# dt in the state-space scan of the feed-forward stage: three exact bf16 parts stacked in 96 partitions and spread by one bf16 product, in place of one f32 product

## Chip, cores and metric

The kernel runs on one core of a Trainium2 chip. The time is the device time of one launch in microseconds (us); of the kernel before there are three runs, and one more execution that the hardware profiler recorded. A lower time is better.

## What is computed

The program is a two-layer post-norm decoder on four sequences of 512 positions and 512 features. Each layer has a mixer, a cross step and a feed-forward part, each followed by a layer norm. Two things matter here: the gated feed-forward part of layer 0 and the selective scan in the cross step of layer 1. The scan doesn't depend on layer 0's feed-forward part, so the kernel runs the two in one stage.

```python
def _L0_ffn_ref(x, w_gate, w_up, w_down):
    gate = jnp.einsum('bsd,hd->bsh', x, w_gate)
    up = jnp.einsum('bsd,hd->bsh', x, w_up)
    gated = jax.nn.silu(gate) * up
    return jnp.einsum('bsh,dh->bsd', gated, w_down)

def _L1_xattn_ref(hidden_states, z, ...):
    ...
    dt = jax.nn.softplus(dt + dt_proj_b[None, :, None])
    A = -jnp.exp(A_log)
    ...
    def step(state, inp):
        d, b, c, u = inp
        dA = jnp.exp(d[..., None] * A)
        state = state * dA + (d * u)[..., None] * b[:, None, :]
        y = jnp.einsum('bdn,bn->bd', state, c)
        return (state, y)
    ...
    y = y + D[None, :, None] * x
    y = y * silu(z)
    return jnp.swapaxes(y, 1, 2)
```

In the scan there are 512 channels, 16 states for each, and 512 positions. dt is f32, all other factors of the scan too.

## The kernel before

A batch is a sequence of blocks; between two of them stands a barrier of all engines, and at the end of some groups of blocks their semaphores are cleared. Everything but the scan's own operations and the spreads is computed with products of bf16 halves: `product` (lines 297, 300 and 301) multiplies high by high, high by low and low by high.

The block that the change touches is `hidden_and_scan`. It is built nine times: once at the start for a scan alone, in each batch once as `ffn` (16 hidden tiles, and the scan of layer 1, `which == 1`), once as `moe` (33 hidden tiles, in three of them with the scan of layer 0 for the next batch). In the `ffn` block the 512 channels of the scan are J = 4 column blocks of 128 partitions. A step s takes 32 of these channels: rows 32 (s % 4) and on, of column block s // 4. There are 16 of them (`blocks`), numbered from 0. 32 channels by 4 states fill the 128 partitions, and the other 4 states lie in the free dimension (GRP = 4), so a step's operations are 128 x 2048.

What a step of the scan does, by engine and line:

- TensorE spreads 32 rows over 128 partitions by a product with a 0/1 pattern (`headmean`, which holds 1/16; the 16 is taken back in scale factors): `spread_dt` (L876) for dt and `spread_dtx` (L889) for dt times x. Both are f32 products with 32 rows of contraction. L876 writes `dt_bank`, L889 writes `dtx_bank`.
- ScalarE (`decays`, L997) makes four exponentials of 511 columns from `dt_bank` into one of two `da` buffers, with the state's rate as scale.
- VectorE (`inputs`, L1054) multiplies the spread dtx by the B rows, and `scan` (L1064) runs the recurrence over 128 x 2048.
- GpSimd (L1154) multiplies the scanned states by the C rows. Each fourth step TensorE sums over the states (`reduce_quad`, L898) and VectorE takes the sum (`finish_y`, L1069).

Beside it a step does one hidden tile: TensorE's `gate` and `up` (12 bf16 products each), ScalarE's tanh (`gate_curve`, L1022), and on VectorE the gate (L1074), times up (L1082) and the low half (`low_part`, L283). From step 4 on TensorE adds a `down_piece` of 12 products, and VectorE takes it out of its bank (`take_down`, L1102 and L1105). All but the last four pieces use the one bank 7, so a piece waits until the one before is taken.

The order on TensorE is written out by hand:

```python
for step in range(steps):
    if 2 <= step + 1 < blocks:
        spread_dtx(step + 1)
    if step + 2 < blocks and not carried:
        spread_dt(step + 2)
    ...
    if step + 1 < tiles:
        gate(step + 1)
        up(step + 1)
```

then `reduce_quad` and the down piece. The dt spread of step s waits for the exponentials of s - 1 (`decay`), since there is one bank for it; the dtx spread waits for the inputs of s - 1 (`inp`). ScalarE's exponentials for step s wait until scan s - 2 is over. VectorE's order in a step is scan, inputs of the next step, the down piece, `finish_y`, gate, times up, low half. Ahead of the loop VectorE splits x into halves (L283, four operations) and makes the inputs of step 0. SP does one thing here: it loads weight slots into a ring of three (L168), each as soon as a slot is free.

Of the kernel before, what the change touches and what calls it, by code (L numbers as in the profile page):

```python
# [285 lines left out]
def halves(region):  # L286

    return region.bitcast(BF16)
# [21 lines left out]
def stream_block(k, sp, slots_end, last=NSLOTS):  # L310
    k.w.load_until(sp, slots_end, RING - 1, last)
# [474 lines left out]
def hidden_and_scan(nc, k, tag, tiles, slot, which, gated, last, splitter=None, early=()):  # L786
# [14 lines left out]
    with ExitStack() as ctx:  # L801
# [41 lines left out]
        def quartet(s):  # L843
            return states(s).rearrange("p (n t) -> p n t", n=GRP)

        carried = gated and blocks > 0
        made = 1 if carried else 0

# [13 lines left out]

        @blk.sync
        def _(sp):
            stream_block(k, sp, slot + (hidden_slots(tiles) if tiles else 0), last)
            if splitter:
                splitter.move(sp)

        @blk.tensor
        def _(pe):  # L870
            def spread_dt(s):

                if s >= 1:
                    pe.wait_ge(decay, s)
                at = slice(32 * (s % 4), 32 * (s % 4) + 32)
                pe.matmul(dt_bank, k.headmean[at, :], dt[at, s // 4, :], start=True, stop=True).then_inc(dt_mm, 1)  # L876

# [107 lines left out]
        def _(act):  # L985
# [29 lines left out]
            def gate_curve(jt):  # L1015
# [5 lines left out]
                else:  # L1021
                    act.activation(t2[jt % 2], gate_bank(jt), ACT.Tanh, scale=0.5).then_inc(th, 1)  # L1022

            if blocks and not made:
                decays(0)
            if tiles:
                gate_curve(0)
            for step in range(steps):
# [19 lines left out]
        def _(dve):  # L1048
# [60 lines left out]
            if tiles and not gated:  # L1109
                for c in range(KM):  # L1110
                    low(dve, xlo[:, c, :], k.xr[:, c, :]).then_inc(xsplit, 1)
            if blocks:
                inputs(0)
            for step in range(steps):
                if step < blocks:
                    scan(step)
                    for n in split_now(step, 1):
                        if not splitter.by_pe(n):
                            splitter.low_part(dve, n)
                if step + 1 < blocks:  # L1120
                    inputs(step + 1)
                if LAG <= step < pieces + LAG:
                    take_down(step - LAG)
                if step % 4 == 1 and 5 <= step <= blocks + 1:
                    finish_y(step // 4 - 1)
                if step < tiles and not gated:
                    silu_gate(step)
                if step < tiles:
                    times_up(step)
                if gated and step < tiles:  # L1130
                    times_weight(step)
                if step < tiles:
                    low_part(step)
                if carried and step == 1:
                    half = slice(J // 2, J)
                    dve.tensor_tensor(dt[:, half, :], dt[:, half, :], dtx[:, half, :], ALU.add).then_inc(late_sum, 1)
                if which == 0 and step % 4 == 2 and step + 2 < blocks:
                    inputs_of(step // 4 + 1)
# [973 lines left out]
def set_constants(nc, k, params_src, squares_src, loads):  # L2112

    with ExitStack() as ctx:
# [25 lines left out]
        def _(dve):  # L2140
# [2 lines left out]
                dve.tensor_copy(k.key_rows_b[:, q, :], k.key_rows[q])  # L2143
            dve.tensor_scalar(k.minus, k.ident, -1.0, None, ALU.mult)
            dve.tensor_scalar(k.stack, k.headmean[:, 0:32], 16.0, None, ALU.mult)
            dve.tensor_copy(k.identb, k.ident).then_inc(neg, 1)
            dve.wait_ge(rate, 1)
            dve.tensor_scalar(k.a0, k.a0, -16.0, None, ALU.mult)
# [31 lines left out]
def decoder(nc, xT, guwT, ctxT, wstream, params, squares, out):  # L2180

    with ExitStack() as ctx:
# [63 lines left out]
        k.ident, k.meanmat, k.headmean = [k.squares[:, i, :] for i in range(3)]  # L2246
        k.key_sum, k.key_rows = [[k.squares[:, 3 + 2 * i + q, :] for q in range(2)] for i in range(2)]
        k.identb = sb("identb", [P, P], BF16)
        k.stack = sb("stack", [P, 32], BF16)
        k.minus = halves(k.held[:, 0, 0:P // 2])  # L2250
        def param(name):
# [228 lines left out]
```

## Time and profile before

| | before |
|---|---|
| median of three runs | 3989.97 us (3979.78 to 3990.33) |
| the profiled execution's own time | 3982.17 us |
| its span, first to last instruction | 3980.4 us |
| mean granted TensorE clock | 0.939 of full speed |
| busy share: TensorE, VectorE, ScalarE, GpSimd | 88%, 80%, 40%, 35% |
| matmuls recorded | 15,442 |

The profile gives for each instruction its start and duration, and in brackets the idle time of its engine before it with what ended that. Matmuls overlap (the next starts before the last ends), so for TensorE the distance from start to start is what one costs, and the end of its records is modelled. An f32 product appears as two records. The engines' queues run in the order of the program; a wait holds up what stands behind it on that engine.

### The profile page before, as it was taken

To read this page: it belongs to the slowest core of one execution; us is meant where nothing else is said; L and a number is where in the kernel's file an instruction comes from. 1 tells how busy PE (TensorE), PEld (TensorE's weight loads), DVE (VectorE), ACT (ScalarE), POOL (GpSimd) and SP (SyncE) were. 2 spreads that over 40 slices of the span, in tenths; PEclk is the share of its full clock that TensorE was granted. 3 is DMA by queue.
4 is the path that set the end of the run, shared out by engine and by line. 5 is a ranking of instruction groups with operands and counts; after the bars stand their busy time and mean duration, and the time that the engine had idled before them with its cause. 6 is when DMAs were issued, how large, how long until landed. Compare 5 with 4: busy or idle time off the path is not lost. (4 is left out here: it accounts for less than half of the span.)

```text
span 3980.4 us, 41707 instructions
## 1 busy us (share of the span) xinstructions
PE 3521.7 (88%) x15442; PEld 1475.8 (37%) x15442; DVE 3172.7 (80%) x2733; ACT 1609.0 (40%) x2189; POOL 1378.0 (35%) x493
## 2 busy tenths in 40 slices
PE   5777779989999979989999979989999988967999
PEld 1222243334333443334333443334433443324444
DVE  5999469887999869887999869887999869895333
ACT  5666343214655353214655353214655343213001
POOL 3454304362344304372344304372344304361000
PEclk9788899999899999989899999989899999978999
DMA  6678402121233302122233302122233302110222
GB/s 228 241 286 302 159 12 72 60 78 65 88 105 97 131 27 72 59 72 72 85 102 102 130 27 72 57 74 72 79 104 105 131 27 72 57 40 16 103 96 72
DMA packets 105431, 382.95 MB, mean 96 GB/s; under 512 B 14224, under 2 KB 27920, under 8 KB 102800
## 3 DMA queue, kind: packets, MB, share of 16 engines
q1 hardware_dynamic: 83632, 342.57, 24.6%
q10 hardware_dynamic: 21600, 37.73, 3.4%
q8 instruction: 125, 2.05, 0.2%
q14 instruction: 74, 0.61, 0.1%
HBM read 290.80 MB, written 64.32 MB: 89 GB/s over the span
## 5 line engine op out<-in xcount | busy, mean ns | idle before, releaser
L300 PE MATMUL ps<-r,ring 128*128 128x512 bf16 (+1 forms) x2040 | 781.4, 384 | 0.0
L297 PE MATMUL ps<-xr,ring 128*128 128x512 bf16 x1568 | 613.8, 391 | 1.4 <-PEq L2278 1.4
L301 PE MATMUL ps<-xr,ring 128*128 128x512 bf16 x1568 | 611.1, 390 | 0.0
L297 PE MATMUL ps<-r,ring 128*128 128x512 bf16 (+3 forms) x1384 | 545.4, 395 | 49.4 <-DVE xc L1102 17.8
L301 PE MATMUL ps<-r,ring 128*128 128x512 bf16 (+3 forms) x1384 | 544.8, 395 | 0.0
L1154 POOL TENSOR_TENSOR hh<-hh,bc 128x2048 f32<-128x2048 f32 x72 | 334.7, 4649 | 518.3 <-DVE hh L1064 518.3
L1154 POOL TENSOR_TENSOR bc<-bc 128x2048 f32<-128x2048 f32 x64 | 304.3, 4754 | 344.6 <-DVE bc L1064 344.6
L1154 POOL TENSOR_TENSOR r<-r,bc 128x2048 f32<-128x2048 f32 x56 | 260.9, 4658 | 297.7 <-DVE r L1064 297.7
L1064 DVE TENSOR_TENSOR_SCAN hh<-da,hh 128x2048 f32<-128x2048 f32 x72 | 325.7, 4523 | 1.3
L1105 DVE TENSOR_TENSOR xc<-xc,ps 128x512 f32<-128x512 f32 x176 | 119.5, 679 | 226.1 <-PE ps L301 225.8
L1064 DVE TENSOR_TENSOR_SCAN bc<-da,bc 128x2048 f32<-128x2048 f32 x64 | 296.0, 4625 | 0.5
L300 PEld LDWEIGHTS ps<-r,ring 128*128 128x128 bf16 (+1 forms) x2040 | 196.9, 97 | 246.2 <-issue 13.2
L1064 DVE TENSOR_TENSOR_SCAN r<-da,r 128x2048 f32<-128x2048 f32 x56 | 261.0, 4660 | 0.6
L997 ACT ACTIVATE da<-da,params_sb 128x511 f32<-128x511 f32 x372 | 248.0, 714 | 31.0 <-DMA da<-r 23.9
L297 PEld LDWEIGHTS ps<-xr,ring 128*128 128x128 bf16 x1568 | 151.8, 97 | 271.6 <-issue 106.5
L997 ACT ACTIVATE da<-ps,params_sb 128x511 f32<-128x511 f32 x384 | 231.8, 692 | 23.4 <-DVE r L1064 10.1
L297 PEld LDWEIGHTS ps<-r,ring 128*128 128x128 bf16 (+3 forms) x1384 | 134.0, 97 | 284.8 <-issue 136.1
L301 PEld LDWEIGHTS ps<-xr,ring 128*128 128x128 bf16 x1568 | 151.4, 97 | 208.0 <-issue 6.4
L307 PE MATMUL ps<-identb 128*128 128x512 bf16 x748 | 183.0, 401 | 30.9 <-ACT r L1427 22.1
L997 ACT ACT_TABLE_LOAD x98 | 125.7, 1283 | 198.7 <-issue 178.0
L301 PEld LDWEIGHTS ps<-r,ring 128*128 128x128 bf16 (+3 forms) x1384 | 134.4, 97 | 186.2 <-issue 11.7
L889 PE MATMUL ps<-ctxTs,squares_sb 32*128 32x512 f32 x256 | 153.8, 682 | 52.5 <-DVE ctxTs L1058 21.8
(267 smaller groups left out, 6559.4 us busy)
## 6 DMA issues: line engine op xcount, KB each, us to landing
ring<-wsplit SPq DMA_DIRECT2D x216, 768.0 KB, 4.2
r<-wstream SPq DMA_DIRECT2D x54, 768.0 KB, 7.0
ring<-wsplit SPq DMA_DIRECT2D x76, 512.0 KB, 3.9
wsplit<-ring SPq DMA_DIRECT2D x38, 768.0 KB, 4.3
da<-r ACTq DMA_DIRECT2D x360, 63.9 KB, 2.1
wsplit<-r SPq DMA_DIRECT2D x14, 768.0 KB, 5.5
r<-wstream SPq DMA_DIRECT2D x19, 512.0 KB, 6.4
r<-xT SPq DMA_DIRECT2D x7, 1024.0 KB, 6.4
```

The costliest lines, as they stand in the source:

```text
L297: mm = pe.matmul(out, w_hi, x_hi, start=start, stop=False)
L300: pe.matmul(out, w_hi, x_lo, start=False, stop=False)
L301: return pe.matmul(out, w_lo, x_hi, start=False, stop=stop)
L307: pe.matmul(k.ps[:, bank, :], k.identb, k.identb[:, None, :].broadcast_to([P, 4, P]), start=True, stop=True)
L889: pe.matmul(dtx_bank, k.headmean[at, :], source, start=True, stop=True).then_inc(dtx_mm, 1)
L997: return act.activation(k.da[s % 2][:, n, 1:T], source, ACT.Exp, scale=rate[:, GRP * s + n:GRP * s + n + 1])
L1064: dve.tensor_tensor_scan(states(s), k.da[s % 2][:, :, :].rearrange("p n t -> p (n t)"), states(s), 0.0, ALU.mult, ALU.add).then_inc(scanne ...
L1105: dve.tensor_tensor(k.xc[:, m, :], k.xc[:, m, :], down_bank(p), ALU.add).then_inc(taken, 1)
L1154: pool.tensor_tensor(quartet(s), quartet(s), k.out_rows, ALU.mult).then_inc(read, 1)
```

## The change

In the `ffn` block alone (`stacked`), dt of the column blocks 1 to 3 (steps 4 to 15) is split into three bf16 parts whose sum is the f32 value. ScalarE copies it to bf16, VectorE subtracts that in place from dt, ScalarE copies the rest to bf16, VectorE subtracts again, and the last rest is the third part. SP then issues twelve transfers within SBUF that lay the three parts of each group of 32 rows under each other in 96 partitions (`dt_stack`). From step 4 on `spread_dt` is one bf16 product over these 96 rows with a bf16 copy of the pattern. The first four steps keep their f32 product. SP's stream of weights is cut in two around the transfers. `dt_parts` and `dt_stack` lie in a region that is free in this block.

```diff
@@ hidden_and_scan
+        stacked = which == 1
+        dt_parts, stack_in = sem("dt_parts"), sem("stack_in")
         carried = gated and blocks > 0
...
         @blk.sync
         def _(sp):
+            if stacked:
+                stream_block(k, sp, slot + 1, last)
+                sp.wait_ge(dt_parts, 4)
+                for i in range(3):
+                    for c in range(4):
+                        sp.dma_start(k.dt_stack[32 * i:32 * i + 32, :, c, :], k.dt_parts[32 * c:32 * c + 32, i, :, :]).then_inc(stack_in, 16)
             stream_block(k, sp, slot + (hidden_slots(tiles) if tiles else 0), last)
...
             def spread_dt(s):
                 if s >= 1:
                     pe.wait_ge(decay, s)
+                if stacked and s >= 4:
+                    if s == 4:
+                        pe.wait_ge(stack_in, 12 * 16)
+                    pe.matmul(dt_bank, k.headmean_b[0:96, :], k.dt_stack[:, s // 4 - 1, s % 4, :], start=True, stop=True).then_inc(dt_mm, 1)
+                    return
                 at = slice(32 * (s % 4), 32 * (s % 4) + 32)
                 pe.matmul(dt_bank, k.headmean[at, :], dt[at, s // 4, :], start=True, stop=True).then_inc(dt_mm, 1)
...
+            if stacked:
+                act.activation(k.dt_parts[:, 0, :, :], dt[:, 1:J, :], ACT.Copy).then_inc(dt_parts, 1)
             if blocks and not made:
                 decays(0)
+            if stacked:
+                act.wait_ge(dt_parts, 2)
+                act.activation(k.dt_parts[:, 1, :, :], dt[:, 1:J, :], ACT.Copy).then_inc(dt_parts, 1)
             if tiles:
                 gate_curve(0)
...
+            if stacked:
+                dve.wait_ge(dt_parts, 1)
+                dve.tensor_tensor(dt[:, 1:J, :], dt[:, 1:J, :], k.dt_parts[:, 0, :, :], ALU.subtract).then_inc(dt_parts, 1)
             if blocks:
                 inputs(0)
+            if stacked:
+                dve.wait_ge(dt_parts, 3)
+                dve.tensor_tensor(k.dt_parts[:, 2, :, :], dt[:, 1:J, :], k.dt_parts[:, 1, :, :], ALU.subtract).then_inc(dt_parts, 1)
             for step in range(steps):
@@ set_constants, decoder
+            dve.tensor_copy(k.headmean_b, k.headmean)
...
+        k.headmean_b = sb("headmean_b", [P, P], BF16)
+        k.dt_parts = halves(r0[:, 1536:3840]).rearrange("p (i j t) -> p i j t", i=3, t=T)
+        k.dt_stack = halves(r0[0:96, 8192:11264]).rearrange("p (j c t) -> p j c t", c=4, t=T)
```

How it moves the queues. In the rows below L numbers of the changed program are its own: L902 is the old L889, L886 the new product, L1072 and L1082 are the old L1054 and L1064, L1010 is the old L997.

ScalarE, start of the `ffn` block (`da` are the decays, `row` and `r0` behind L1022/L1035 the tanh), before:

```order
L984 UNCONDITIONAL_BRANCH
L997 ACT_TABLE_LOAD
L997 ACTIVATE da0<-ps,params_sb 128x511 x4
L1022 ACTIVATE row<-ps 128x512
L997 ACTIVATE da1<-ps,params_sb 128x511 x4
```

and in the change:

```order
L997 UNCONDITIONAL_BRANCH
L1038 ACTIVATE r0<-r1 128x1536
L1010 ACT_TABLE_LOAD
L1010 ACTIVATE da0<-ps,params_sb 128x511 x4
L1043 ACTIVATE r0<-r1 128x1536
L1035 ACTIVATE row<-ps 128x512
L1010 ACTIVATE da1<-ps,params_sb 128x511 x4
```

The first copy stands ahead of the table load, the second between the first four exponentials and the first tanh.

VectorE at the same place (`hh0` is the first states buffer; the scan stands as SCALAR_TENSOR_TENSOR), before:

```order
L1047 UNCONDITIONAL_BRANCH
L283 TENSOR_TENSOR r0<-xr 128x512 x4
L1054 TENSOR_TENSOR hh0<-ps,bc 128x2048
L1064 SCALAR_TENSOR_TENSOR hh0<-da0,hh0 128x2048
L1054 TENSOR_TENSOR hh1<-ps,bc 128x2048
```

and in the change:

```order
L1065 UNCONDITIONAL_BRANCH
L283 TENSOR_TENSOR r0<-xr 128x512 x4
L1132 TENSOR_TENSOR r1<-r1,r0 128x1536
L1072 TENSOR_TENSOR hh0<-ps,bc 128x2048
L1137 TENSOR_TENSOR r0<-r1,r0 128x1536
L1082 SCALAR_TENSOR_TENSOR hh0<-da0,hh0 128x2048
L1072 TENSOR_TENSOR hh1<-ps,bc 128x2048
```

One subtraction stands ahead of the inputs of step 0 and one between them and the first scan.

TensorE at the top of step 2 of the first `ffn` block, before:

```order
L301 MATMUL ps<-xr,ring 128x512
L889 MATMUL ps<-r,squares_sb 128x512
L876 MATMUL ps<-r,squares_sb 128x512
L297 MATMUL ps<-xr,ring 128x512
L300 MATMUL ps<-r,ring 128x512
```

and in the change:

```order
L301 MATMUL ps<-xr,ring 128x512
L902 MATMUL ps<-r,squares_sb 128x512
L886 MATMUL ps<-r,headmean_b 128x512
L297 MATMUL ps<-xr,ring 128x512
L300 MATMUL ps<-r,ring 128x512
```

The new product stands where the f32 one stood, behind the dtx spread and ahead of the gate tile; so it is in each of the steps 2 to 13.

## Rows read from the trace of the kernel before

**Rows 1.** Timeline, VectorE, start of the second ffn block; columns: start, duration, engine, line, shapes

```profile
1497.09 2.50 DVE L283 TENSOR_TENSOR r<-xr 128x512 bf16<-128x512 f32 x4 [2.28 <-PEq L2278]
1500.87 2.29 DVE L1054 TENSOR_TENSOR hh<-ps,bc 128x2048 f32<-128x2048 f32 x1 [1.29 <-PE ps L889]
1503.27 4.42 DVE L1064 TENSOR_TENSOR_SCAN hh<-da,hh 128x2048 f32<-128x2048 f32 x1
```

**Rows 2.** Timeline, ScalarE, the same place

```profile
1497.05 1.28 ACT L997 ACT_TABLE_LOAD   x1 [4.26 <-PEq L2278]
1499.17 2.42 ACT L997 ACTIVATE da<-ps,params_sb 128x511 f32<-128x511 f32 x4 [0.83 <-PE ps L876]
```

**Rows 3.** Timeline, VectorE, steps 1 and 2: inputs, and the two low halves

```profile
1518.11 2.29 DVE L1054 TENSOR_TENSOR bc<-ps,bc 128x2048 f32<-128x2048 f32 x1 [0.86 <-PE ps L889]
...
1521.75 0.69 DVE L283 TENSOR_TENSOR held_first<-r 128x512 bf16<-128x512 f32 x1
...
1530.31 1.67 DVE L283 TENSOR_TENSOR held_first<-r 128x512 bf16<-128x512 f32 x1
```

**Rows 4.** Timeline, GpSimd, steps 1 and 2

```profile
1517.32 4.57 POOL L1154 TENSOR_TENSOR hh<-hh,bc 128x2048 f32<-128x2048 f32 x1 [4.96 <-DVE hh L1064]
1526.86 4.58 POOL L1154 TENSOR_TENSOR bc<-bc 128x2048 f32<-128x2048 f32 x1 [4.97 <-DVE bc L1064]
```

**Rows 5.** Timeline, TensorE, its waits for VectorE in steps 4, 6 and 7

```profile
1538.56 0.69 PE L889 MATMUL ps<-r,squares_sb 32*128 32x512 f32 x1 [0.87 <-DVE r L1054]
...
1568.14 0.39 PE L297 MATMUL ps<-r,ring 128*128 128x512 bf16 x1 [0.49 <-DVE xc L1102]
...
1577.70 0.39 PE L297 MATMUL ps<-r,ring 128*128 128x512 bf16 x1 [0.23 <-DVE xc L1102]
```

**Rows 6.** Timeline, VectorE, its waits in steps 9 and 13

```profile
1594.44 2.29 DVE L1054 TENSOR_TENSOR r<-ps,bc 128x2048 f32<-128x2048 f32 x1 [0.56 <-PE ps L889]
...
1634.76 2.29 DVE L1054 TENSOR_TENSOR bc<-ps,bc 128x2048 f32<-128x2048 f32 x1 [1.70 <-PE ps L889]
```

**Rows 7.** Timeline, TensorE, a stand in the mixing block and that of step 15

```profile
948.87 0.39 PE L297 MATMUL ps<-r,ring 128*128 128x512 bf16 x1 [2.08 <-POOL held_first L283]
...
1654.94 0.39 PE L297 MATMUL ps<-r,ring 128*128 128x512 bf16 x1 [2.96 <-DVE xc L1105]
```

**Rows 8.** Timeline, TensorE, both spreads in step 6 and the next product

```profile
1561.08 0.69 PE L889 MATMUL ps<-r,squares_sb 32*128 32x512 f32 x1
1561.09 0.69 PE L876 MATMUL ps<-r,squares_sb 32*128 32x512 f32 x1
...
1562.14 0.40 PE L297 MATMUL ps<-xr,ring 128*128 128x512 bf16 x1
```

**Rows 9.** Timeline, TensorE, mixture stage: dtx alone, a 96-row bf16 product, the next

```profile
1984.43 1.12 PE L889 MATMUL ps<-ctxTs,squares_sb 32*128 32x512 f32 x2
1985.49 0.39 PE L943 MATMUL ps<-r,stack 96*128 96x512 bf16 x1
1985.72 0.39 PE L297 MATMUL ps<-xr,ring 128*128 128x512 bf16 x1
```

**Rows 10.** One line's instructions, durations in ns min/median/max: copies and subtractions up to 1,536 columns

```profile
L260 ACT ACTIVATE ring<-r x52: 622/1475/1527, 12.7 to 420.9; 128x1536 bf16<-128x1536 f32 x38, 128x1024 bf16<-128x1024 f32 x11, 128x1152 bf16<-128x1152 f32 x1, 128x512 bf16<-128x512 f32 x1
...
L265 DVE TENSOR_TENSOR r<-r x5: 1192/1726/1727, 129.3 to 376.7; 128x1536 bf16<-128x1536 f32 x4, 128x1024 bf16<-128x1024 f32 x1
```

**Rows 11.** Timeline, TensorE, both spreads in step 2

```profile
1523.84 0.69 PE L889 MATMUL ps<-r,squares_sb 32*128 32x512 f32 x1
1524.24 0.69 PE L876 MATMUL ps<-r,squares_sb 32*128 32x512 f32 x1
```

**Rows 12.** Stretches: length, busy PE, PEld, DVE, ACT, POOL, granted clock, DMA share, GB/s

```profile
1655.70:1658.90 3.20, 3.20 (x9) 1.03 (x8) 3.17 (x2) 0.00 (x0) 3.13 (x1) 0.50 0.58 177
...
949.10:952.40 3.30, 3.30 (x9) 1.12 (x8) 3.30 (x4) 0.00 (x0) 2.67 (x3) 0.50 0.58 194
```

**Rows 13.** Timeline, SP, eight transfers of 32 rows within SBUF

```profile
1907.46 5.03 SPq L1843 DMA_DIRECT2D da<-r  x8
```

## Prediction

> **What bounds the kernel now.** I read the page's busy shares first, then the timelines of single engines in the second batch's feed-forward stage (1497 to 1674 us), then the granted clock by stretches. The shares have TensorE and VectorE both high, and in this stage both are nearly full, so they don't say on which of the two a microsecond counts. The timelines do. The program has four batches with one such stage each, and what is worked out for one is taken four times.
>
> At the start VectorE splits x until 1499.59, idles 1.29 us for the dtx spread, makes the inputs at 1500.87 and starts its first scan at 1503.27 [rows 1]. ScalarE's four exponentials are done by 1501.59 [rows 2].
>
> In steps 0 to 4 VectorE and GpSimd set the pace. In step 1 VectorE waits 0.86 us for TensorE's spread, in step 2 it doesn't, yet the remainder (line 283) ends 5.12 us after the start of GpSimd's product in both: 1522.44 against 1517.32, 1531.98 against 1526.86 [rows 3, 4]. GpSimd starts when the scan ends and its 4.57 us close the step; without a wait the remainder only stands longer (1.67 us instead of 0.69). The Trainium skill says so of this pair (SBUF — State Buffer, section "SBUF: two separate sides"): the port pair that they share is an exclusive lock, held for a whole instruction. The trace agrees. So a later first scan is not won back from that 0.86 us.
>
> TensorE is early by then: in step 4 it waits 0.87 us for VectorE's inputs, until 1538.56. In steps 6 and 7 it waits for the down bank, 0.49 and 0.23 us by the brackets, which is 0.66 and 0.41 against the regular 0.22 us between bf16 starts; the last such wait ends at 1577.70 [rows 5]. From there TensorE runs without a gap and VectorE waits for its dtx spread, 0.56 us in step 9 and 1.70 us in step 13 [rows 6]. Then VectorE leads: TensorE stands 2.96 us, until 1654.94, for VectorE to take the piece before [rows 7], and runs the last pieces. The stage's end is thus a chain: VectorE's first scan; VectorE's pace to 1577.70; TensorE's pace to step 13; VectorE's pace to 1654.94; TensorE's rest.
>
> **The spread that is replaced costs nothing.** In a steady step dtx (L889) and dt (L876) start at 1561.08 and 1561.09, and the next bf16 product at 1562.14: 1.06 us for both [rows 8]. In the mixture stage, where only dtx is spread, it takes 1.06 us too: 1984.43 to 1985.49 [rows 9]. The two read different groups of 32 rows and run side by side. The bf16 product over 96 rows that comes in has its like right there: L943, 96 rows, behind a lone dtx, 0.23 us to the next start at 1985.72 [rows 9]. So dtx plus bf16 dt is 1.29 where dtx plus f32 dt was 1.06: **TensorE loses 0.23 us in a steady step**. Bounds: 0 (it runs beside dtx after all) and 0.5 (half of the pair's 1.06).
>
> Which of the twelve count? Those of steps 2 and 3 come before TensorE's wait of step 4. That of step 13 comes before its 2.96 us stand. Those of steps 4 to 7 are counted below. Those of steps 8 to 12 lie on TensorE's stretch of the chain: 5 x 0.23 = 1.15 us.
>
> **The split at the start.** ScalarE now copies 1,536 columns ahead of its table load; this copy takes 1.48 us in the weight split [rows 10]. 1497.05 + 1.48 + 1.28 + 2.42 = 1502.23 [rows 2], second copy to 1503.71. VectorE gets one subtraction of 1,536 columns before the inputs and one after, 1.73 us each at that length [rows 10]: 1499.59 + 1.73 + 2.29 = 1503.61, a wait to 1503.71, + 1.73 = 1505.44, where the scan starts instead of at 1503.27. **2.15 us per stage**; by VectorE's sum alone, 3.46 added less 1.29 idle filled, 2.17. Bounds: 1.7 (queued instructions overlap) and 2.8 (three handovers at 0.2 more). TensorE needs none of it before step 2, and from step 4 on waits for VectorE's inputs, so the whole 2.15 goes through.
>
> **The wait that grows.** TensorE's steps 1 to 3 do not move, so its wait in step 4 becomes 0.87 + 2.15 = 3.0 us, and 0.3 more since the 0.40 us by which dt now starts late in steps 2 and 3 [rows 11] no longer lengthens the pair. After the 2.96 us stand at the end the granted clock reads 0.50, the lower of the two levels (1.2 GHz), from 1655.7 to 1658.9; after a 2.08 us idle at 948.87 it is 0.50 from 949.1 to 952.4 [rows 7, 12]. So I expect this level after step 4 as well, for the same 3.3 us. At half clock 3.3 us do the work of 1.65: TensorE is 1.65 late. The bf16 dt adds 0.23 in each of steps 4 to 7, 0.92, less 0.3 in step 4, where dt starts late on its wait as in step 2. Against this stand the losses of steps 5 to 7, 0.22 (too small to be listed), 0.66 and 0.41: 1.65 + 0.92 - 0.3 - 1.29 = 1.0 us late at the start of TensorE's stretch. Bounds: 0 (clock stays up; the 0.6 left is covered) and 2.0. VectorE's two waits grow by it: 0.56 to 1.7 in step 9, and together by 2.1 at step 13.
>
> **The transfers.** SP waits for the fourth count (1505.4), then issues 12 transfers. Eight of its 32-row transfers take 5.03 us to issue [rows 13]: 12 x 0.63 = 7.6, to 1513.0. I give 2 to 4 us for landing; TensorE wants them at 1524.24 [rows 11]. Slack of 7 us or more: nothing. Behind the waiting SP stands the next weight load; its slot comes free only in step 0 of TensorE and its tile is used two steps later, so a microsecond there costs nothing.
>
> Elsewhere a 128x128 copy among the constants and one more semaphore clear at some group ends: 0.4 us in all, a guess, bounds 0 and 1.
>
> **Sum.** Per stage 2.15 + 1.15 + 1.0 = 4.3; 4 x 4.3 + 0.4 = 17.6. The profiled execution took 3982.17 us and would take 3999.8. It is 7.8 below the median of the three runs, 3989.97, which spread over 10.5 us. On the median: **4007.6 us**, +0.44%. A measurement tells about 0.3%, 12 us, from no change.
>
> **Rivals.**
> - *The clock stays up in step 4.* Then 4 x 3.3 + 0.4 = 13.6, 4003.6. For it: a wait of 0.87 there leaves no trace. Against: rows 7 and 12. Chance 0.15.
> - *One price only.* If the 0.23 is hidden beside dtx and the clock stays: 4 x 2.15 + 0.4 = 9.0, 3999.0. If the later scan is swallowed by VectorE's waits of 0.86, 0.56 and 1.70: 5.0, 3995.0. Against: the equal 5.12 us of rows 3 and 4, and that the later two waits are for TensorE, which itself follows VectorE in step 4. Chance 0.14.
> - *The other side: the f32 spread was not free.* If the pair's costs add up in the steps that count, a dt product falls from 1.06 to 0.23, 0.83 less: 4.15 per stage over five steps, 10 over all twelve. Less 2.15: -2.0 or -7.8 per stage, 3982.0 or 3958.8. It decides once dt beyond dtx costs over 0.23 + 2.15 / 5 = 0.66 us. For it: in step 2 dt starts 0.40 us behind dtx [rows 11]; nothing waits for that. Against: rows 8 and 9. The Trainium skill (FP8 and Floating Point Precision, section "TensorE Precision Notes") has true FP32 at 4 passes through the array. By that rule, as an estimate, three passes of 0.22 are saved, 0.67 x 5 less 2.15, the stage gains 1.2 and the time is 3985; it counts passes, not what runs beside them. Chance 0.05.
> - *The stack comes late.* Its runs of 1 KB go to few rows while weights are in flight. Beyond 7 us of delay each further microsecond is paid in each stage, once step 4's wait of 3 us is used up: 13 us late is 4 x 3 = 12 more, 4020. Chance 0.08.
>
> **Chances.** The forecast has the rest, 0.58, all but 0.06 of it beyond 12 us. First rival 0.10 slower, 0.05 same. Second 0.14 same. Third 0.04 faster, 0.01 same. Fourth 0.08 slower. Sums: slower 0.70, same 0.26, faster 0.04. The range reaches down to one price and an execution as low as the profiled one (3993) and up by the bounds of the start (2.8) and of the clock (2.0) to 4017.
>
> **What would show it.** Right: first scan of each stage 2.1 us later against the stage's start; L902/L886 1.29 us to the next product; step 1 without its wait, step 13's at 3.8 us; a granted clock of 0.50 in step 4 behind an idle of 3 us. Wrong: L886 starting with L902; a stage no longer than now; TensorE idle in step 2.

## The result, and the profile after

The change is slower. Its median over five runs is 4012.14 us (4005.19 to 4017.06) against 3989.01 us of five runs of the kernel before (3979.78 to 3990.33): a ratio of 1.0062, 95% interval 1.0044 to 1.0080. 4007.6 was forecast, with a range from 3993 to 4017.

| | after |
|---|---|
| the profiled execution's own time, its span | 4012.14 us, 4010.4 us |
| mean granted TensorE clock | 0.933 |
| busy share: TensorE, VectorE, ScalarE, GpSimd | 89%, 80%, 40%, 34% |
| matmuls recorded | 15,394 |

The timeline of VectorE at the start of the second `ffn` block, which answers [rows 1]:

```profile
1509.72 2.50 DVE L283 TENSOR_TENSOR r<-xr 128x512 bf16<-128x512 f32 x4 [2.28 <-PEq L2306]
1512.13 1.75 DVE L1132 TENSOR_TENSOR r<-r 128x1536 f32<-128x1536 f32 x1
1513.80 2.28 DVE L1072 TENSOR_TENSOR hh<-ps,bc 128x2048 f32<-128x2048 f32 x1
1516.32 1.76 DVE L1137 TENSOR_TENSOR r<-r 128x1536 bf16<-128x1536 f32 x1 [0.23 <-ACT r L1043]
1517.99 4.42 DVE L1082 TENSOR_TENSOR_SCAN hh<-da,hh 128x2048 f32<-128x2048 f32 x1
```

The first scan stands 8.27 us behind the start of the block, where it stood at 6.18: 2.09 later, in all four stages.

The same place on ScalarE (answers [rows 2]):

```profile
1509.70 1.48 ACT L1038 ACTIVATE r<-r 128x1536 bf16<-128x1536 f32 x1 [4.28 <-PEq L2306]
1511.20 1.28 ACT L1010 ACT_TABLE_LOAD   x1
1512.49 2.42 ACT L1010 ACTIVATE da<-ps,params_sb 128x511 f32<-128x511 f32 x4
1514.79 1.50 ACT L1043 ACTIVATE r<-r 128x1536 bf16<-128x1536 f32 x1
```

The copies take 1.48 and 1.50 us, near the 1.475 of [rows 10]; the second ends after VectorE's inputs and makes it wait 0.23 us. SP's queue issues the transfers right after (answers [rows 13]):

```profile
1518.11 8.36 SPq L872 DMA_DIRECT2D r<-r  x12
```

TensorE: the first new product, in step 2, and a wait in step 3, both of the second `ffn` block; then step 4 of the first and of the second block (answers [rows 5] and [rows 8]):

```profile
1537.54 0.39 PE L886 MATMUL ps<-r,headmean_b 96*128 96x512 bf16 x1
...
1543.73 1.12 PE L902 MATMUL ps<-r,squares_sb 32*128 32x512 f32 x2 [0.47 <-DVE bc L1072]
...
649.35 1.12 PE L902 MATMUL ps<-r,squares_sb 32*128 32x512 f32 x2 [2.73 <-DVE r L1072]
650.40 0.39 PE L886 MATMUL ps<-r,headmean_b 96*128 96x512 bf16 x1
650.63 0.39 PE L297 MATMUL ps<-xr,ring 128*128 128x512 bf16 x1
...
1553.25 1.12 PE L902 MATMUL ps<-r,squares_sb 32*128 32x512 f32 x2 [2.74 <-DVE r L1072]
```

The pair takes 1.05 + 0.23 = 1.28 us to the next product, where it took 1.06. The first new product starts at 1537.54 behind its dtx spread, with no wait in brackets; the last of the transfers was issued by 1526.47, and each landed 2.1 to 2.9 us after it was issued: the stack is not late. The stand of step 4 grew from 0.87 to 2.74 in the second block, and step 3, which had no wait there, now waits 0.47. Behind the stand of step 4 the granted clock falls in the first, third and fourth block, not in the second. Stretches just behind the two stands (columns as in [rows 12]):

```profile
650.00:653.40 3.40, 3.40 (x11) 1.14 (x10) 3.37 (x3) 0.00 (x0) 1.73 (x1) 0.67 0.38 99
...
1553.90:1557.30 3.40, 3.40 (x16) 1.36 (x15) 3.37 (x3) 0.00 (x0) 1.74 (x1) 1.00 0.40 90
```

VectorE's waits in steps 9 and 13 of the first block (0.57 and 1.70 there before, as in the second block in [rows 6]):

```profile
706.36 2.29 DVE L1072 TENSOR_TENSOR r<-ps,bc 128x2048 f32<-128x2048 f32 x1 [1.71 <-PE ps L902]
...
747.52 2.29 DVE L1072 TENSOR_TENSOR bc<-ps,bc 128x2048 f32<-128x2048 f32 x1 [2.56 <-PE ps L902]
```

I cut both programs at the starts of their blocks, the first VectorE instruction behind each barrier. The four stages, in us:

| | start to first scan | first to last scan | from there to the end | stage |
|---|---|---|---|---|
| before, each of four | 6.18 | 146.54 to 146.57 | 24.98 | 177.70 to 177.73 |
| after, batch 1 | 8.27 | 148.48 | 24.74 | 181.49 |
| batch 2 | 8.27 | 147.59 | 24.93 | 180.79 |
| batch 3 | 8.27 | 148.50 | 24.79 | 181.56 |
| batch 4 | 8.27 | 148.47 | 24.55 | 181.29 |

The stages hold 14.3 us of the change (725.1 against 710.9); 17.2 was forecast. The spans differ by 30.0. The rest, 15.7, lies outside these stages, where the change adds only a 128x128 copy among the constants and a semaphore clear at some group ends. The experiments are about both parts.

### The profile page after: what moved, and what is told of

Same layout as the page of the kernel before. It is cut to its first block and busy times, and to the rows that moved or that the text cites. A ratio compares the mean times of both kernels' runs of the same rounds, so it can differ in the third digit from the quotient of the medians.

```text
span 4010.4 us, 41698 instructions
## 1 busy us (share of the span) xinstructions
PE 3556.4 (89%) x15394; PEld 1487.1 (37%) x15394; DVE 3200.1 (80%) x2742; ACT 1620.4 (40%) x2197; POOL 1344.6 (34%) x493
## 5 line engine op out<-in xcount | busy, mean ns | idle before, releaser
L1082 DVE TENSOR_TENSOR_SCAN hh<-da,hh 128x2048 f32<-128x2048 f32 x72 | 325.6, 4522 | 0.8
L1082 DVE TENSOR_TENSOR_SCAN bc<-da,bc 128x2048 f32<-128x2048 f32 x64 | 296.1, 4627 | 0.5
L1082 DVE TENSOR_TENSOR_SCAN r<-da,r 128x2048 f32<-128x2048 f32 x56 | 260.8, 4657 | 0.6
L1010 ACT ACTIVATE da<-da,params_sb 128x511 f32<-128x511 f32 x372 | 248.0, 714 | 25.5 <-DMA da<-r 18.6
L1010 ACT ACTIVATE da<-ps,params_sb 128x511 f32<-128x511 f32 x384 | 231.8, 691 | 26.9 <-DVE bc L1082 14.5
L301 PEld LDWEIGHTS ps<-r,ring 128*128 128x128 bf16 (+3 forms) x1384 | 134.9, 98 | 187.7 <-issue 14.3
L902 PE MATMUL ps<-ctxTs,squares_sb 32*128 32x512 f32 x256 | 153.2, 680 | 54.1 <-DVE ctxTs L1076 25.5
```

The source lines that it names most:

```text
L301: return pe.matmul(out, w_lo, x_hi, start=False, stop=stop)
L902: pe.matmul(dtx_bank, k.headmean[at, :], source, start=True, stop=True).then_inc(dtx_mm, 1)
L1010: return act.activation(k.da[s % 2][:, n, 1:T], source, ACT.Exp, scale=rate[:, GRP * s + n:GRP * s + n + 1])
L1082: dve.tensor_tensor_scan(states(s), k.da[s % 2][:, :, :].rearrange("p n t -> p (n t)"), states(s), 0.0, ALU.mult, ALU.add).then_inc(scanne ...
```

## The experiments

"Stages" is the sum of the four stages in the run's own profile, less the 710.9 us of before; it comes from one execution of each kernel. The ratio is against executions of the kernel before on the same chip, whose medians were 3989.18 (e1 to e4), 3989.54 (e5 to e8) and 3987.49 us (e9 to e12).

| run | median, us | ratio, 95% interval | stages, us |
|---|---|---|---|
| e1 split only | 3996.28 | 1.0018, 1.0010 to 1.0027 | +8.8 |
| e2 product only | 3990.88 | 1.0004, 0.9996 to 1.0012 | +8.3 |
| e3 transfers only | 3997.65 | 1.0024, 1.0014 to 1.0033 | +0.2 |
| e4 the change again | 4011.22 | 1.0062, 1.0047 to 1.0078 | +15.8 |
| e5 no dt product | 3984.82 | 0.9990, 0.9981 to 0.9998 | 0.0 |
| e6 both on one group of rows | 4015.53 | 1.0062, 1.0047 to 1.0076 | +23.9 |
| e7 change, stand filled | 3999.77 | 1.0026, 1.0017 to 1.0035 | +12.6 |
| e8 pair early | 3981.87 | 0.9984, 0.9974 to 0.9994 | -3.0 |
| e9 change, no transfers | 4019.15 | 1.0068, 1.0047 to 1.0088 | +14.5 |
| e10 cut only | 3995.26 | 1.0018, 1.0009 to 1.0028 | 0.0 |
| e11 before again | 3988.65 | 1.0002, 0.9993 to 1.0010 | +0.2 |
| e12 pair early, stand filled | 3981.89 | 0.9985, 0.9977 to 0.9994 | -3.5 |

### The parts of the change: e1 to e4

**e1**, the change without transfers and bf16 product; every spread is f32 and reads what the subtraction left.

```diff
-            if stacked:
-                stream_block(k, sp, slot + 1, last)
-                sp.wait_ge(dt_parts, 4)
...
-                if stacked and s >= 4:
...
-                    return
```

> The changed kernel with the two copies and two subtractions left in, but without the transfers, and with the f32 spread of dt back in steps 4 to 15 (it reads what the subtraction left, so the decays are of a rest and not of dt). Theory: first scan of each stage 2.1 us later, TensorE idle 2.7 us in step 4, granted clock 0.50 behind it in most stages (0.9 us more by step 13), scans 0 to 15 together 146.6 or 147.4 us; against before 4 x 2.1 to 4 x 3.0, +8 to +12 us, 0.2 to 0.3%. Rival (the split is swallowed by VectorE's waits): scan 15 no later against the stage's start, +0. Rival (there is a cost outside the stages): blocks between the stages longer than in the kernel before by 10 us in sum.

The first scans stand at 8.27 us as in the change. The scans take 146.90, 146.56, 146.89 and 146.91 us: the fall of the clock behind step 4 is there in three stages, and costs 0.35 where the bf16 product doesn't add to it. The down-bank waits of steps 6 and 7 take up the rest of it.

**e2**, the kernel before with a bf16 product of 96 rows (high halves of dt, so other values are spread) from the product for step 4 on.

```diff
+                if which == 1 and s >= 4:
+                    pe.matmul(dt_bank, k.headmean_b[0:96, :], high(dt[0:96, s // 4, :]), start=True, stop=True).then_inc(dt_mm, 1)
+                    return
```

> The kernel before with one edit: from step 4 on the spread of dt is a bf16 product over 96 rows, of the high halves of whatever lies there (so the decays are wrong ones); no split, no transfers. Theory (the f32 spread was free beside dtx): dtx and dt together 1.29 us instead of 1.06; VectorE's wait in step 13 at 2.7 us instead of 1.7; 1.05 us per stage, +4.2 us, 0.1%. Rival (the f32 spread was paid): stage shorter by 3 us or more, -12 us. Rival (the bf16 product runs beside dtx): no change.

The scans take 148.57 to 148.62 us in three stages, 2.0 more (150.27 in the first), where 1.05 was forecast. VectorE's waits in steps 9 and 13 of the second block are 1.65 and 2.60. The forecast had left out the clock: it falls behind step 4's stand here too, and in all four stages, though the stand is only 1.22 to 1.32 us in three of them (1.84 in the first). The second block:

```profile
1547.10 1.12 PE L892 MATMUL ps<-r,squares_sb 32*128 32x512 f32 x2 [1.24 <-DVE r L1057]
...
1547.90:1551.30 3.40, 3.40 (x9) 1.16 (x9) 3.37 (x3) 0.00 (x0) 1.58 (x1) 0.53 0.33 99
```

So 2.0 is the 1.05 us that the product takes with the clock up (second stage of the change) and about 1.0 for the clock. In the first stage the clock stays low for 6.6 us in place of some 3.3, which gives the 1.7 more. Each of e1 and e2 has a fall of the clock of its own behind step 4, and the change has only one; so their stage costs, 8.8 and 8.3, don't add up to those of the change. The whole run shows nothing of the 8.3: by the medians it is 1.7 us slower than before, with an interval that ends at 1.0012 (4.8 us). Why the rest of this kernel is cheaper in most executions is not known.

**e3**, the kernel before with twelve transfers of the same size behind the first inputs, and TensorE waiting for them at the product for step 4.

```diff
+            if stacked:
+                stream_block(k, sp, slot + 1, last)
+                sp.wait_ge(inp, 1)
+                for i in range(3):
+                    for c in range(4):
+                        sp.dma_start(k.dt_stack[32 * i:32 * i + 32, :, c, :], dt[32 * c:32 * c + 32, 1:4, 128 * i:128 * i + T // 2]).then_inc(stack_in, 16)
...
+                if stacked and s == 4:
+                    pe.wait_ge(stack_in, 12 * 16)
```

> The kernel before with twelve transfers within SBUF of the same shape and size as in the change, at the same time in the stage, and TensorE's wait for them at the dt spread of step 4; nothing reads what they write. Theory: hidden, all scans at the same distances as before, +0 (within 3 us). Rival (transfers or the SP queue cost time, by late weights or inside VectorE's work): +2 us or more per stage, 8 us in all, with TensorE or VectorE waiting in step 2 or 3.

From the first scan on no scan moves by 0.1 us, as expected (the first scan itself stands 0.35 us later in one stage and 0.35 earlier in another), yet the run is 8.5 us slower by the medians, with an interval that excludes nothing happening. At +0 to 3 us this forecast failed, and e9 to e11 follow it up.

**e4**, the changed kernel once more, unchanged.

> The changed kernel once more, unchanged. The stages differ by 14.3 us between the two profiled executions and what lies between the stages by 15.7, in work that the change doesn't touch. Theory (the granted clock ahead of the stages falls differently from execution to execution): the stages again 180.8 to 181.6 us each, but the rest anywhere within 3269 to 3285 us. Rival (the change makes the rest longer): the rest again 3283 to 3287.

The ratio repeats. Its stages took 182.59, 180.84, 181.55 and 181.68 us: the clock stayed up in the second again, and stayed low for longer in the first. The rest took 3276.5 us, against 3285.2 in the change's own profile: the theory, that the rest differs from execution to execution, holds, and its rival (3283 to 3287) falls. This execution, 4004.95 us, is the lowest of its six.

### Was the f32 product free? e5 and e6

**e5**, the kernel before without the dt product from step 4 on.

```diff
+                if which == 1 and s >= 4:
+                    return
...
-                act.wait_ge(dt_mm, s + 1)
+                act.wait_ge(dt_mm, min(s + 1, 4) if which == 1 else s + 1)
```

> The kernel before, with no dt spread at all from the product for step 4 on (ScalarE's exponentials of these steps read the values that the bank still holds, so the output is not the reference's). Theory: dtx and the f32 dt product run side by side, so the f32 dt product costs nothing beyond dtx: a lone dtx to the next product is 1.06 us as before, the stage keeps its 177.7 us within 0.3 us and the time is that of before, +0 to -2 us. Rival (the f32 product is not free): each of the 10 products of steps 4 to 13 gives back up to 0.83 us, those of steps 8 to 12 on TensorE's stretch 4 us per stage, time -8 to -16 us.

**e6**, the kernel before with the dt product on the same 32 rows as the dtx product ahead of it.

```diff
+                if which == 1 and s >= 4:
+                    at = slice(32 * ((s - 1) % 4), 32 * ((s - 1) % 4) + 32)
```

> The kernel before, with the f32 dt product from the one for step 4 on reading the same group of 32 rows as the dtx product ahead of it (so dt of other channels is spread and the output is not the reference's). Theory: the overlap of the pair comes from its two different groups of rows; on one group they run one behind the other, the pair takes about 2.1 us instead of 1.06, and the stage grows by about as much as for five to ten products: the scans, 146.5 us from the first to the last before, take 5 to 9 us more per stage, time +20 to +36 us. Rival (the overlap has another reason, or dt has another price than the chain says): pair stays at 1.06 us and the time is that of before.

TensorE in step 6, e5 first:

```profile
1561.06 1.12 PE L891 MATMUL ps<-r,squares_sb 32*128 32x512 f32 x2
1562.11 0.40 PE L297 MATMUL ps<-xr,ring 128*128 128x512 bf16 x1
```

and e6:

```profile
1566.08 1.12 PE L891 MATMUL ps<-r,squares_sb 32*128 32x512 f32 x2
1567.04 1.02 PE L878 MATMUL ps<-r,squares_sb 32*128 32x512 f32 x2
1567.99 0.40 PE L297 MATMUL ps<-xr,ring 128*128 128x512 bf16 x1
```

dtx alone takes 1.05 us, the pair on two groups of rows 1.06 [rows 8], the pair on one group 1.91. With no dt product at all, every stage keeps its 177.72 or 177.73 us. But that equal length is in part luck. Without the product TensorE is at step 4 earlier, stands 1.66 us there in place of 0.87, and the clock falls behind it in all four stages. The second block of e5:

```profile
1538.40:1541.80 3.40, 3.40 (x9) 1.16 (x9) 3.37 (x3) 0.00 (x0) 1.41 (x1) 0.52 0.49 134
```

TensorE is then 1.3 us behind the kernel before at its next dtx spread, and catches up by step 8, since it has no wait in steps 6 and 7 any more. What shows the price is TensorE's own stretch behind that: from the dtx spread of step 8 to that of step 14 it takes 62.31 us before (1580.45 to 1642.76) and 62.27 in e5 (1579.38 to 1641.65), with six f32 dt products between them or none. Together with e6 this settles it for the steps that count: the product that the change replaces cost nothing, and because it ran on other rows than dtx. e6's 0.85 us a step is 6.1 us a stage. By its median e5 is 4.7 us faster than before, where 0 to 2 was expected; its stages give none of it.

### The clock behind step 4: e7

**e7**, the change with 12 products on bank 7 that only keep TensorE busy, in step 4 ahead of its dtx spread.

```diff
+                if stacked and step == 4:
+                    keep_busy(k, pe, 7, 12)
```

> The changed kernel with 12 small products that only keep TensorE busy, in step 4 ahead of its dtx spread, where TensorE stands 2.73 us for VectorE's inputs. Theory: the stand is what brings the granted clock down behind it in three of the four stages (scans 148.5 us against 147.6 in the stage where it stayed up); without the stand the clock stays at 1.00 there, the scans take 147.6 us in all four stages and the time falls by 3 x 0.9 = 2.7 us, 0 to -6 us measured. Rival (the clock falls there by itself, or its fall is covered by later waits): scans stay at 148.5, time as that of the change, +22 us against before.

The first block of e7, TensorE's timeline in step 4:

```profile
641.20 2.75 PE L307 MATMUL ps<-identb 128*128 128x512 bf16 x12
644.11 1.12 PE L902 MATMUL ps<-r,squares_sb 32*128 32x512 f32 x2 [0.15 <-DVE r L1074]
```

and the stretch behind it, where the change had 0.67:

```profile
645.00:648.40 3.40, 3.40 (x16) 1.46 (x16) 3.37 (x3) 0.15 (x1) 1.49 (x1) 1.00 0.45 125
```

All four stages take 180.87 to 180.89 us, the scans 147.61 to 147.63. So the fall costs 0.9 us a stage where it happens in the change. The split and the product are 2.09 + 1.07 by themselves. But the median fell by 11.4 us against e4, where 0 to 6 was expected, and the stages hold 3.2 of it. The other 8 lie outside again.

### Outside the stages: e9, e10, e11

**e9**, the change with its bf16 product reading the first part where ScalarE wrote it, and no transfers.

```diff
-                        pe.wait_ge(stack_in, 12 * 16)
-                    pe.matmul(dt_bank, k.headmean_b[0:96, :], k.dt_stack[:, s // 4 - 1, s % 4, :], start=True, stop=True).then_inc(dt_mm, 1)
+                        pe.wait_ge(dt_parts, 4)
+                    pe.matmul(dt_bank, k.headmean_b[0:96, :], k.dt_parts[0:96, 0, s // 4 - 1, :], start=True, stop=True).then_inc(dt_mm, 1)
```

> The change without its twelve transfers: the bf16 product of 96 rows reads the first part where ScalarE put it (so dt of wrong rows is spread and the output is not the reference's). In the stages nothing should differ from the change: first scan at 8.27 us, scans 147.6 us where the clock stays up and 148.5 us where it falls behind step 4's stand, together 14 to 16 us more than before. Theory A (the transfers of the change cost nothing on their own, what lies outside the stages comes from the granted clock of each execution): time within 4 us of the change's, +18 to +22 us against before. Theory B (the transfers cost 8 us, as the run with transfers alone says): 8 us less than the change, +13 to +15 us.

**e10**, e3 without its transfers and without TensorE's wait: SP's cut and its wait are left, and the constant.

```diff
+            if stacked:
+                stream_block(k, sp, slot + 1, last)
+                sp.wait_ge(inp, 1)
```

> The kernel before with SP's stream of weights cut in two and SP waiting for the first inputs in between, as in the run with transfers alone, but with no transfer and no wait on TensorE. If the 8.5 us of that run come from the cut, the wait or the added constant, they are here too (+8 us); if they come from the transfers, this kernel has the time of before (+0 us, within 4).

**e11**, the kernel before, unchanged.

> The kernel before, unchanged, for a second profile and for what the comparison makes of no change. Theory (blocks outside the feed-forward stages differ from execution to execution by steps of 1.8 and 3.2 us, with the granted clock): the four stages take 177.7 us each again, some other blocks differ from the first profile by such steps, and the ratio is 1.000 with an interval of about 0.001 to either side. Rival (an execution of one program repeats its blocks, so differences outside the stages belong to the kernel that shows them): all blocks within 0.3 us of the first profile.

Theory B falls: without its transfers the change is no faster. Theory A doesn't hold in its numbers either: e9 should have been 18 to 22 us slower than before, and is 31.7 by the medians, 7 above the change. Its six executions spread over 22 us (4002.73 to 4024.70), and its stages hold 14.5. And the 8 us of e3 are in e10, which moves no transfer. Where do they go? In e11 the stages are those of the first profile within 0.15 us, most blocks within 0.1, but the three before the first `ffn` block are 2.53, 1.33 and 3.31 us longer. Four others differ by 0.8 to 2.3 us, up and down, and nearly cancel. The theory behind e11 holds in this: the blocks move in steps, and with the granted clock; the steps are 1.3, 2.5 and 3.3 us there. The second of the three as a stretch (start:end, length, then as in [rows 12]), in the first profile of before:

```profile
556.20:574.00 17.80, 9.77 (x62) 5.57 (x63) 12.65 (x32) 8.94 (x17) 0.02 (x1) 1.00 0.00 0
```

and in e11:

```profile
557.90:577.00 19.10, 11.79 (x61) 6.97 (x63) 12.65 (x32) 8.92 (x17) 0.02 (x1) 0.82 0.00 0
```

e11's own time, 3989.28, is near before's median, and the change's profiled execution is its median. So these two are the pair to compare: spans 22.9 apart, the medians 23.1. Stages 14.1; the mixture blocks 3.5 (2.1, 0.7, 1.4 and -0.8); the two blocks before the last `ffn` block 5.4. That last place in e11 and in the change:

```profile
3256.40:3274.20 17.80, 9.72 (x62) 5.56 (x64) 12.65 (x33) 8.93 (x17) 0.03 (x1) 1.00 0.01 1
3274.20:3299.80 25.60, 14.29 (x61) 8.36 (x61) 17.59 (x25) 16.20 (x24) 0.36 (x1) 0.83 0.00 0
```

```profile
3270.90:3290.50 19.60, 13.42 (x62) 7.19 (x62) 12.91 (x32) 8.95 (x17) 0.00 (x0) 0.74 0.00 1
3290.50:3319.80 29.30, 17.58 (x61) 10.74 (x61) 17.77 (x25) 16.20 (x24) 0.40 (x1) 0.72 0.00 0
```

In e10 and e3 it is the last mixture block that is longer, by 3.1 us. So it is in e4 (138.8 us against 135.7 in e11), though not in the change's own profile (135.0), which is the same program. Six-us stretches in it, e11 and e10:

```profile
3514.00:3520.00 6.00, 6.00 (x24) 2.23 (x23) 6.00 (x8) 1.18 (x2) 6.00 (x4) 0.82 0.30 117
3520.00:3526.00 6.00, 6.00 (x28) 2.43 (x27) 5.28 (x7) 0.60 (x2) 4.78 (x5) 1.00 0.36 131
3526.00:3532.00 6.00, 5.83 (x27) 2.25 (x27) 6.00 (x8) 3.49 (x7) 3.57 (x3) 1.00 0.16 31
```

```profile
3515.00:3521.00 6.00, 6.00 (x24) 2.26 (x23) 6.00 (x8) 1.20 (x2) 6.00 (x4) 0.85 0.30 115
3521.00:3527.00 6.00, 6.00 (x21) 2.35 (x19) 4.86 (x6) 0.00 (x0) 4.78 (x5) 0.72 0.39 131
3527.00:3533.00 6.00, 5.66 (x21) 1.94 (x21) 4.98 (x7) 1.74 (x3) 2.37 (x3) 0.78 0.00 0
```

Up to the first of the three both are alike; then e11's clock is back at 1.00 and e10's stays low for some 18 us more. So, in these pairs of profiles, what a kernel pays outside the stages is how long the granted clock stays low at such places. Part of that is chance, since it differs between executions of one program. Part seems to belong to the kernel, since e10's interval, 1.0009 to 1.0028 over 12 runs, leaves 1 out. What in e10 sets it (the cut, SP's wait or the constant) wasn't taken apart and stays open.

### A faster version: e8 and e12

**e8**, the kernel before with the pair of spreads of steps 9 and 13 issued ahead of the sum over states in steps 8 and 12.

```diff
+                early_pair = which == 1 and step in (9, 13)
-                if 2 <= step + 1 < blocks:
+                if 2 <= step + 1 < blocks and not early_pair:
                     spread_dtx(step + 1)
-                if step + 2 < blocks and not carried:
+                if step + 2 < blocks and not carried and not early_pair:
                     spread_dt(step + 2)
...
+                if which == 1 and step in (8, 12):
+                    spread_dtx(step + 2)
+                    spread_dt(step + 3)
                 if step % 4 == 0 and 4 <= step <= blocks:
                     reduce_quad(step // 4 - 1)
```

> The kernel before, with the dtx and dt spreads of steps 9 and 13 issued one piece earlier on TensorE, ahead of the sum over states and the down piece of steps 8 and 12. Theory: VectorE's waits of 0.56 us in step 9 and 1.70 us in step 13 are waits for these spreads, on the chain; without them VectorE is ahead and the stage ends up to 2.26 us earlier, time -4 to -9 us. Rival (TensorE's total work sets step 13 to 15 anyway, so what VectorE saves it waits for the down bank or for gate and up): the waits move, the stage keeps 177.7 us, time +0.

e8 is faster than both kernels, 0.9984 of before. The stages give 3.0 us of it. The waits of [rows 6] left step 9 and shrank to 0.39 us in step 13, and most of them came back in steps 10 and 14, as the rival had it. VectorE's timeline in the second block:

```profile
1609.95 2.29 DVE L1058 TENSOR_TENSOR r<-ps,bc 128x2048 f32<-128x2048 f32 x1 [0.22 <-PE ps L889]
...
1650.55 2.29 DVE L1058 TENSOR_TENSOR bc<-ps,bc 128x2048 f32<-128x2048 f32 x1 [1.33 <-PE ps L889]
```

Of 2.26 us 0.43 is won. TensorE's stand of step 15 is 1.92 us in all four stages, where it was 2.96. Behind it the clock stays up in three of them, which gives another 0.43 each; in the first it falls all the same:

```profile
763.90:767.10 3.20, 3.20 (x9) 1.14 (x8) 3.13 (x3) 0.00 (x0) 3.20 (x1) 0.51 0.45 151
```

**e12**, e8 with that stand filled.

```diff
+                if which == 1 and step == 15:
+                    pe.wait_ge(decay, 16)
+                    keep_busy(k, pe, 0, 12)
```

> The kernel before with the pair of spreads early in steps 8 and 12, and with 12 products that only keep TensorE busy in step 15, in the 2.96 us in which it stands for VectorE's take of the down bank. Theory: the granted clock stays at 1.00 behind that stand instead of 0.50 for 3.3 us, each stage ends up to 1.6 us earlier on top of the 0.4 to 0.9 us that the early pair brings: stages about 175.3 us, time -12 to -16 us against before. Rival (VectorE, not TensorE, ends the stage, or the clock falls later instead): stages 176.9 us, time as with the early pair alone, -4 to -8 us.

The clock stays up in all four stages, and each takes 176.81 to 176.85 us, no less than e8's best (176.82). The rival was right in effect, though with another engine: TensorE in step 15 of e8,

```profile
1660.54 0.39 PE L297 MATMUL ps<-r,ring 128*128 128x512 bf16 x1 [1.92 <-DVE xc L1109]
1664.50 0.62 PE L898 MATMUL ps<-hh,squares_sb 128*32 128x512 f32 x2 [1.13 <-POOL bc L1158]
```

With the clock up TensorE is through its piece early and waits 1.13 us for GpSimd's last product. The low clock was hidden behind GpSimd but for 0.43 us.

## Why the prediction was right, and where not

The direction, the three terms of the stage and their places came out. The total, 4012.14, lies in the range, but 8.8 us of it come from a place that the forecast had at 0.4. The range left room for them only because it was wide for other reasons (the start and the clock of step 4), and that is luck. By the bounds that the prediction names, the range would be 3991.2 to 4014.2 and not 3993 to 4017; the result lies in both. Step by step:

- *The split at the start*, 2.15 forecast: 2.09 in each stage of the change, e1 and e7. The second copy made VectorE wait 0.23 us, where 0.10 was forecast. Nothing later won the 2.09 back.
- *The spread that is replaced costs nothing*: e5 and e6 show it, and why. 1.29 against 1.06 was forecast for the pair, 1.28 measured. In steps 2 to 4, where it starts late, the f32 product did hold TensorE up, but ahead of waits that took it in. The product's term was 1.15; it is 1.05 in the second block of the change, 1.07 in e7. The rival that has the f32 product not free is out. The Trainium skill (FP8 and Floating Point Precision, section "TensorE Precision Notes") counts 4 passes for true FP32. One alone takes 1.05 us here and a bf16 product 0.23, 4.6 times less, which is near that count. But the count says nothing of a neighbour on other rows, and the 3985 us by it had the wrong sign.
- *The wait that grows*: 3.0 and 0.3 more was forecast for step 4, with steps 1 to 3 of TensorE unmoved. It is 2.74 there in the second block and 0.47 in step 3, 3.2 together: the sum was right, its place not wholly. VectorE's wait in step 1 is gone, as forecast.
- *The clock*: 1.0 in each stage was forecast; it was 0.9 in three of four stages, and none in the second. The same stand of 2.7 us precedes all four, so its length doesn't decide alone. The other runs say so too: in step 4 the clock fell behind 1.22 us (third block of e2) and not behind 1.34 (first block of e3). The forecast took the fall from what followed stands of 2.08 and 2.96 us; what decides it stays open. VectorE's two waits grew by 2.0 us where the clock fell; 2.1 was forecast in the sum. In the list of what would show it I had put step 13 alone at 3.8 us; it reads 2.56. That line contradicted the sum, which had it right.
- *The transfers*: hidden. 8.36 us of issue for 7.6, 2.1 to 2.9 us of landing for 2 to 4, no wait on TensorE, and e9 is no faster without them.
- *The end of the stage*, which the forecast left as it was: from the last scan to the end the four stages are 0.9 us shorter together (24.98 before, 24.55 to 24.93 now). That is why they hold 14.3 us and not 4 x (2.09 + 1.05) + 3 x 0.9 = 15.3.
- *Elsewhere 0.4 us, a guess, bounds 0 and 1*: this is the step that was mis-sized. Between two executions whose times are near the medians, e11's and the change's, 8.8 us are lost outside the stages, in stretches of low granted clock. Of one pair alone this says little: e4's execution loses nothing there against e11's (3276.5 us both), and is 7 us below the change's median. But over all executions the medians lie 23 us apart and the stages hold 14 to 16, so 7 to 9 is the usual loss. I also took the profiled execution as a fair base and only scaled to the median, though it lay 7.8 us under it. e11 lies 7.1 us above it, and the three blocks before the first stage, with their lower clock, make up 7.2.

So 17.2 + 0.4 was forecast, and 14.1 + 8.8 happened. The stage was 3.1 us too dear and the rest 8.4 too cheap; by the medians that is 0.44% forecast and 0.58% measured (the ratio above says 0.62%).

What stays open: why the change pays more outside than e7, which only adds twelve products in step 4. The stages explain 3.2 of 11.4 us. That the filled stand also spares the blocks behind it is the obvious reading, but e5 and e10, whose stages are exactly those of before, lie at 0.9990 and 1.0018, so a kernel's place in this range can move with no stand changed. I call it argued, not shown.

## What to carry to other kernels

Before replacing an f32 product by a cheaper bf16 one, look at the distance to the next product with and without it: a product of 32 rows beside another on different rows may cost nothing, and the cheaper one over 96 rows that replaced it here cost 0.23 us at the same place. (That it is paid because its 96 rows take in those of dtx was not tested.) Preparation put ahead of the first scan is paid in full when the engine that it delays leads the stage, as the 2.09 us were here. An equal stage length doesn't show that a product was free: look at the distances on its own engine, as in e5. And take the profile apart by blocks: when a change of 0.2% sits in blocks that were not edited, compare it with a second profile of the same program before giving it a cause.

## What the runs showed of the hardware

- Two f32 products of 32 rows side by side took 1.06 us on different groups of rows, 1.91 us on the same group, one alone 1.05 us.
- TensorE's granted clock fell behind a stand of 2.73 us in step 4 in three stages of four, and not behind the same place filled with 12 further products (e7: 1.00 against 0.67). In step 4 it also fell behind stands of 1.22 to 1.84 us (e2, four stages) and 1.66 to 1.78 us (e5, four stages), and not behind 0.85 to 1.34 us (e3, four stages). In e8 a stand of 1.92 us in step 15 left it at 1.00 in three blocks, and it fell to 0.51 behind the same stand in the first.
- The same instructions in the same block took 17.8 us or 19.0 to 19.6 us, and the next block 25.6 to 29.3 us, longer where the granted clock was lower. Two executions of the kernel before differed by 7.2 us in three such blocks, and two of the changed kernel by 8.7 us outside the stages.
- Kernels whose four stages sum to those of before within 0.2 us (e3, e5, e10) had ratios from 0.9990 to 1.0024 with intervals of 0.001 to either side, while the unchanged kernel gave 1.0002.
